# Two attentions over 77 keys: both kinds of scores in one bank per head, on four strips at a time

## The chip, the cores and the metric

The kernel runs on one core of one Trainium2 chip. The metric is the device time of one execution in microseconds; the time shown is the median of three runs.

## The reference, cut to what matters

A decoder of two layers works on x of 8 x 256 tokens x 256 features, with a context of 8 x 77 tokens. Each layer has a self-attention, an attention over the context and a mixture of experts, each followed by a sum and a layer norm. The change touches only the two attentions over the context, which have 16 heads of 16 features. The first (stage L0x) normalises q and k per head and turns q by position:

```python
q = (x @ q_w.T + q_b).reshape(b, s1, H, hd).transpose(0, 2, 1, 3)
kv = (y @ kv_w.T + kv_b).reshape(b, s2, 2, H, hd).transpose(2, 0, 3, 1, 4)
q = _apply_rope(_layernorm(q, qn_w, qn_b)) * scale
k = _layernorm(k, kn_w, kn_b)
attn = softmax(einsum('bhqd,bhkd->bhqk', q, k))          # 256 x 77 a head
o = einsum('bhqk,bhkd->bhqd', attn, v)
return o.reshape(b, s1, c) @ out_w.T + out_b
```

The second (stage L1x) is the same without the norms, the turning and the biases of q, k and v. All is float32.

## The kernel before, in words

One program runs seven stages one after the other; `context_stage` (line 111) builds both L0x and L1x, its kind "rope" or "cross". A stage works through 8 batch entries (blocks, b), each in four steps (st = 0 to 3) of four heads, so n = 4 b + st runs from 0 to 31. The four heads lie on four strips of 32 partitions: `qs` and `keys` have 16 features and a row for the shift in each strip, and a matmul on one strip uses 32 rows of TensorE's array. Every step computes the scores twice.

`scores(n, pair)` (line 527) gives queries on the partitions and keys along the row, for two heads j in the two banks of `psS`, 2 x 77 columns a head; pair 0 and pair 1 use the two halves of the same two banks. When both are there, `row_max(n)` on VectorE (line 829) takes the maximum of each row, with its sign turned, by one reduction for each pair. TensorE transposes these maxima (the item "top"), and `shift(n)` on VectorE (line 842) adds them to the queries, in the row for the shift. `turned_scores(n, half)` (line 548) then computes keys on the partitions and 256 queries along the row, already less the maximum, for two heads in the two banks of `psK`, and `exponential(n, half)` on ScalarE (line 684) takes them to `pT`. `values(n)` (line 559) multiplies by v and `row_sums(n)` (line 571) by ones, both into the bank `psO`, where two steps share a set of 128 output rows. After the second of them `out_norm(o)` on VectorE (line 848) takes the reciprocal of the sums (line 850) and multiplies (line 854). ScalarE and POOL split the result into two parts (`out_high`, `out_low`) for the output projection.

The work that prepares later blocks and closes earlier ones comes in items, each in one of three banks `psF`: transposed x ("xT"), projections ("q", "k", "v", "qT", "kT"), and the output projection ("out", 0 and 1). `slot(n, half)` (line 222) is an order written out by hand: which items stand in the first and the second half of step n. In L1x the second half of each step has the next block's query projection ("qT", line 429), the first half has "xT" at st 0, output projections at st 2 and 3, and in some blocks keys or v at st 1. In L0x the second halves have a query projection (with a bias by line 464), transposes, a v projection in some blocks, and "xT". With the item "top" a few idle matmuls can be issued (`keep_busy`, line 432). In the last blocks most items fall away.

TensorE's order in step n is: turned_scores(n, 0), items of the first slot, values(n - 1), top(n + 1), scores(n + 2, 0), turned_scores(n, 1), row_sums(n - 1), scores(n + 2, 1), items of the second slot. VectorE's is: items of the first slot, shift(n + 1), out_norm(n/2 - 1) if n is even and at least 2, row_max(n + 2), items of the second slot, layer norm. ScalarE's is: exponential(n, 0), items of the first slot, out_high, exponential(n, 1), items of the second slot. All waits are on semaphores counted: `s_max` counts finished row maxima, `p_exp` finished exponentials, `q_shifted` finished shifts.

Of the kernel before, what the change touches and what calls it, by code (L numbers as in the profile page):

```python
# [11 lines left out]
F32 = mybir.dt.float32  # L12
# [8 lines left out]
P = 128  # L21
B = 8
S = 256
# [87 lines left out]
def context_stage(nc, name, kind, consts, x_in, x_out, w):  # L111
# [16 lines left out]
    with ExitStack() as ctx:  # L128
# [59 lines left out]
        psS = ctx.enter_context(nc.psum_tensor(f"{name}_psS", [P, 2, 512], F32))  # L188
        psK = ctx.enter_context(nc.psum_tensor(f"{name}_psK", [P, 2, 512], F32))
# [10 lines left out]
        s_half, s_ready, s_max, q_shifted = sem("s_half"), sem("s_ready"), sem("s_max"), sem("q_shifted")  # L200
# [223 lines left out]
        def _(pe):  # L424
# [102 lines left out]
            def scores(n, pair):  # L527
                b, st = divmod(n, NST)
                if pair == 0:
                    if rope:  # L530
                        for i in range(min(((b + 1) * CTX - 1) // P, CT - 1) + 1):
                            wait_taken(pe, ("kT",), i)
                        wait_taken(pe, ("qT", st // 2), b)
                    else:
                        wait_taken(pe, ("kT", st, b // 4), 0)
                        wait_taken(pe, ("qT", st), b)
                    if n:
                        pe.wait_ge(s_max, n)
                else:
                    pe.wait_ge(s_half, n + 1)  # L540
                for t in range(TT):
                    for j in (2 * pair, 2 * pair + 1):
                        r = slice(32 * j, 32 * j + 32)
                        last = pe.matmul(psS[:, j % 2, (TT * pair + t) * CTX:(TT * pair + t + 1) * CTX],
                                         qs[r, b % 2, st, t * P:(t + 1) * P], keys[r, st, columns(b)], start=True, stop=True)
                last.then_inc(s_half if pair == 0 else s_ready, 1)

            def turned_scores(n, half):
                b, st = divmod(n, NST)
                if half == 0:  # L550
                    pe.wait_ge(q_shifted, n + 1)
                if n or half:
                    pe.wait_ge(p_exp, 2 * n + half)
                for jj in range(2):
                    r = slice(64 * half + 32 * jj, 64 * half + 32 * jj + 32)
                    last = pe.matmul(psK[0:CTX, jj, 0:S], keys[r, st, columns(b)], qs[r, b % 2, st, :], start=True, stop=True)
                last.then_inc(k_ready, 1)

            def values(n):
                b, st = divmod(n, NST)  # L560
                par = st % 2
                pe.wait_ge(p_exp, 2 * n + 2)
                if par == 0 and n >= 2:
                    pe.wait_ge(o_norm, n // 2)
                wait_taken(pe, ("v", b // 2), 0)
                for j in range(4):
                    pe.matmul(psO[32 * j:32 * j + 32, 0:S],
                              vs[0:CTX, b, 4 * (st // 2) + j, 2 * par:2 * par + 2, :].rearrange("p a e -> p (a e)"),
                              pT[0:CTX, n % 2, j, :], start=(par == 0), stop=False)
# [12 lines left out]
            scores(0, 0)  # L582
            scores(0, 1)
            item(("top",), 0)
            scores(1, 0)
            scores(1, 1)
            for n in range(N):
                st = n % NST
                turned_scores(n, 0)
                for what, b in slot(n, 0):  # L590
                    item(what, b)
                if n:
                    values(n - 1)
                if n + 1 < N:
                    item(("top",), n + 1, (1, 0, 2, 0)[st] if rope else (1, 1 if n >= 4 * NST else 0, 0, 0)[st])
                if n + 2 < N:
                    scores(n + 2, 0)
                turned_scores(n, 1)
                if n:
                    row_sums(n - 1)  # L600
                if n + 2 < N:
                    scores(n + 2, 1)
                for what, b in slot(n, 1):
                    item(what, b)
# [6 lines left out]
        def _(act):  # L611
# [72 lines left out]
            def exponential(n, half):  # L684
                act.wait_ge(k_ready, 2 * n + half + 1)
                if half == 0 and n >= 2:
                    act.wait_ge(r_ready, n - 1)
                act.activation(pT[0:CTX, n % 2, 2 * half:2 * half + 2, :], psK[0:CTX, :, 0:S], ACT.Exp).then_inc(p_exp, 1)
# [29 lines left out]
            for n in range(N):  # L718
                st = n % NST
                exponential(n, 0)  # L720
# [5 lines left out]
                exponential(n, 1)  # L726
# [5 lines left out]
        def _(dve):  # L732
# [96 lines left out]
            def row_max(n):  # L829
# [5 lines left out]
                for half in range(2):  # L835
                    last = dve.tensor_reduce(
                        top[:, n % 2, :, 64 * half + HD:64 * half + 64:32].rearrange("p t j -> p j t"),
                        psS[:, :, TT * CTX * half:TT * CTX * (half + 1)].rearrange("p j (t k) -> p j t k", t=TT),
                        AX_X, ALU.max, negate=True)
                last.then_inc(s_max, 1)  # L840
# [2540 lines left out]
```

## Time and profile before

| | us |
|---|---|
| median of 3 runs | 2387.67 |
| lowest, highest | 2387.26, 2424.44 |
| the profiled execution | 2417.0 |
| its span, first to last instruction | 2415.3 |

The profile is that of one execution, on the only core. TensorE's weight loads (PEld) lie beside its matmuls. A float32 matmul stands in the trace as two records, so x8 in a row are four matmuls. PEclk is the share of its full clock that TensorE was granted, 1.00 for 2.4 GHz and 0.50 for 1.2 GHz. An arrow (`<-`) in brackets names what an instruction waited for last.

### The profile page before, as it was taken

To read this page: it belongs to the slowest core of one execution; us is meant where nothing else is said; L and a number is where in the kernel's file an instruction comes from. 1 tells how busy PE (TensorE), PEld (TensorE's weight loads), DVE (VectorE), ACT (ScalarE), POOL (GpSimd) and SP (SyncE) were. 2 spreads that over 40 slices of the span, in tenths; PEclk is the share of its full clock that TensorE was granted. 3 is DMA by queue.
4 is the path that set the end of the run, shared out by engine and by line. 5 is a ranking of instruction groups with operands and counts; after the bars stand their busy time and mean duration, and the time that the engine had idled before them with its cause. 6 is when DMAs were issued, how large, how long until landed. Compare 5 with 4: busy or idle time off the path is not lost. (4 is left out here: it accounts for less than half of the span.)

```text
span 2415.3 us, 39591 instructions
## 1 busy us (share of the span) xinstructions
PE 2064.4 (85%) x15432; PEld 1484.4 (61%) x15432; DVE 1029.0 (43%) x2387; ACT 843.0 (35%) x2148; POOL 650.3 (27%) x607
## 2 busy tenths in 40 slices
PE   5999966998389999389999987995999997899995
PEld 4666755664368888257777765663666665455553
DVE  2556544665323232245555563564356552111112
ACT  3545432342123232335554542432334331122222
POOL 1333334752421321313332331112000000502222
PEclk9999997997589999699999997996799896899998
DMA  1000001000533421600000001002100007412223
GB/s 58 10 10 19 10 14 59 10 23 10 185 93 97 140 80 34 215 1 1 19 10 10 10 10 57 19 19 87 53 14 28 14 28 261 143 36 44 43 42 94
DMA packets 100031, 127.47 MB, mean 53 GB/s; under 512 B 8682, under 2 KB 86970, under 8 KB 99818
## 3 DMA queue, kind: packets, MB, share of 16 engines
q1 hardware_dynamic: 86554, 107.17, 13.5%
q0 software_dynamic: 13296, 17.77, 4.2%
q8 instruction: 128, 2.10, 0.4%
q14 instruction: 53, 0.43, 0.1%
HBM read 87.12 MB, written 39.89 MB: 53 GB/s over the span
## 5 line engine op out<-in xcount | busy, mean ns | idle before, releaser
L2030 POOL TENSOR_TENSOR L1a_probs<-L1a_probs,L1a_rinv 128x1024 f32<-128x1024 f32 x64 | 121.2, 1894 | 286.9 <-DVE L1a_rinv L2360 286.9
L2027 POOL TENSOR_TENSOR L0a_probs<-L0a_probs,L0a_rinv 128x256 f32<-128x256 f32 (+1 forms) x128 | 103.1, 826 | 219.7 <-DVE L0a_rinv L2360 219.7
L2351 DVE CUSTOM_DVE_ANT_0 L1a_sbias<-L1a_psS,L1a_bias 128x256 f32<-128x256 f32 x256 | 93.2, 421 | 124.0 <-PE L1a_psS L2164 124.0
L2279 ACT ACTIVATE L1a_probs<-L1a_sbias,L1a_nmx 128x256 f32<-128x256 f32 x256 | 126.5, 497 | 40.0 <-DVE L1a_nmx L2351 40.0
L3229 DVE TENSOR_TENSOR moe_h<-moe_h,moe_psU 128x512 f32<-128x512 f32 x55 | 37.8, 688 | 226.4 <-PE moe_psU L3048 200.7
L2784 DVE TENSOR_TENSOR ec_hT<-ec_sg,ec_psU 128x512 f32<-128x512 f32 x64 | 44.0, 688 | 194.3 <-ACT ec_sg L2714 194.3
L2999 POOL DMA_INDIRECT moe_sums<-moe_y,moe_xg x39 | 60.8, 1559 | 234.8 <-DVE moe_y L3241 231.9
L2655 PE MATMUL ec_psA<-ec_wd,ec_hT 128*128 128x256 f32 x512 | 112.6, 381 | 5.2 <-DVE ec_hT L2784 5.2
L2279 ACT ACTIVATE L0a_probs<-L0a_psS,L0a_nmx 128x128 f32<-128x128 f32 (+1 forms) x256 | 104.0, 422 | 36.7 <-DVE L0a_nmx L2342 36.7
L2590 POOL DMA_INDIRECT ec_sums<-ec_yk,ec_token_at x32 | 50.4, 1574 | 228.6 <-ACT ec_yk L2722 223.8
L3070 PE MATMUL moe_psY<-moe_wts,moe_hT 128*128 (+1 forms) x440 | 106.0, 384 | 6.1 <-issue 5.3
L3070 PEld LDWEIGHTS moe_psY<-moe_wts,moe_hT 128*128 128x128 f32 x440 | 84.4, 193 | 41.3 <-issue 32.4
L2655 PEld LDWEIGHTS ec_psA<-ec_wd,ec_hT 128*128 128x128 f32 x512 | 96.6, 190 | 20.1 <-DVE ec_hT L2784 7.3
L1564 ACT ACTIVATE L1s_pT<-L1s_psK 128x1024 f32<-128x1024 f32 x64 | 65.6, 1024 | 106.2 <-PE L1s_psK L1428 106.2
L2643 PE MATMUL ec_psG<-ec_xs,ec_wt 128*128 128x512 f32 x384 | 100.4, 397 | 2.1 <-issue 2.1
L3129 ACT ACTIVATE moe_hT<-moe_psH 128x512 f32<-128x512 f32 x55 | 32.8, 597 | 191.0 <-PE moe_psH L3062 171.4
L2643 PE MATMUL ec_psU<-ec_xs,ec_wt 128*128 128x512 f32 x384 | 98.8, 393 | 0.0
L2342 DVE TENSOR_REDUCE L0a_nmx<-L0a_psS 128x2 f32<-128x256 f32 (+1 forms) x128 | 65.3, 552 | 72.4 <-PE L0a_psS L2161 72.4
L1724 DVE TENSOR_REDUCE L1s_top<-L1s_psS 128x8 f32<-128x2048 f32 x32 | 73.2, 2288 | 32.2 <-PE L1s_psS L1414 32.2
L2367 DVE COPY L1a_pT<-L1a_psT 128x1024 f32<-128x1024 f32 x64 | 78.2, 1222 | 19.9 <-PE L1a_psT L2179 19.9
L2714 ACT ACTIVATE ec_sg<-ec_psG 128x512 f32<-128x512 f32 x64 | 38.3, 598 | 137.4 <-PE ec_psU L2643 133.2
L2051 PE MATMUL L1a_psF<-L1a_xT,L1a_wq 128*128 128x256 f32 x384 | 64.8, 306 | 23.4 <-DVE L1a_xT L2377 17.7
(485 smaller groups left out, 4776.9 us busy)
## 6 DMA issues: line engine op xcount, KB each, us to landing
ec_wg<-in_L_ffn_w_gate SPq DMA_DIRECT2D x8, 1024.0 KB
ec_wu<-in_L_ffn_w_up SPq DMA_DIRECT2D x8, 1024.0 KB
ec_wd<-in_L_ffn_w_down SPq DMA_DIRECT2D x8, 1024.0 KB, 5.6
moe_rows<-blank SPq DMA_DIRECT2D x1, 5070.0 KB, 20.9
moe_xg<-moe_rows SPq DMA_DIRECT2D x39, 130.0 KB, 2.1
moe_wts<-in_L_ffn_e_gate SPq DMA_DIRECT2D x8, 512.0 KB
moe_wts<-in_L_ffn_e_up SPq DMA_DIRECT2D x8, 512.0 KB
moe_wts<-in_L_ffn_e_down SPq DMA_DIRECT2D x8, 512.0 KB
```

Of the source, the lines that this page charges most:

```text
L1564: act.activation(pT[0:KP, n % 2, 2 * half:2 * half + 2, :], psK[0:KP, :, 0:KT * S], ACT.Exp).then_inc(p_exp, 1)
L1724: last = dve.tensor_reduce(top[:, n % 2, :, HD::32].rearrange("p t j -> p j t"), psS[:].rearrange("p j (t k) -> p j t k", t=TT), AX_X, ALU ...
L2027: last = pool.tensor_tensor(v, v, bcast(rinv[:, r, :, t], 2, KEYS[t]), ALU.mult)
L2030: last = pool.tensor_tensor(v, v, bcast(rinv[:, r, :, :].rearrange("p h t -> p (h t)"), 2, S), ALU.mult)
L2051: last = pe.matmul(out, l(a), r(c), start=(start and j + k == 0), stop=(stop and 3 * j + k == n - 1))
L2279: ins = act.activation(probs[:, r, j, at:at + KEYS[t]], src[:, at:at + KEYS[t]], ACT.Exp, bias=nmx[:, r, j, t:t + 1], scale=1.0 if latent ...
L2342: last = dve.tensor_reduce(nmx[:, r, :, t], psS[:, slot:slot + 2, P * t:P * t + KEYS[t]], AX_X, ALU.max, negate=True)
L2351: last = dve.tensor_tensor_reduce(out=sbias[:, g % 2, j, t * S:(t + 1) * S], in0=psS[:, slot + j, t * S:(t + 1) * S], in1=bias[:, 2 * (g % ...
L2367: dve.tensor_copy(pT[:, g % 2, :, :].rearrange("p j (k r c) -> p r (j k) c", r=2, c=64), psT[:, :, 0:PW].rearrange("p r (n c) -> p r n c", ...
L2643: last = pe.matmul(ps[:, i % 2, :], wt[:, a, j, c, i * P:(i + 1) * P], xs[:, b, c, :], start=(n == 0), stop=(n == len(products) - 1))
L2655: last = pe.matmul(psA[:, half, s % 2 * D:(s % 2 + 1) * D], hT[:, i, s * P:(s + 1) * P], wd[:, e % 2, i, :], start=(i == 0), stop=(i == IC ...
L3070: last = pe.matmul(psY[:, 0:D], hT[:, g % 2, f, :], weights(e, 2)[:, f * D:(f + 1) * D], start=(f == 0), stop=(f == FC - 1))
```

## The change

Both stages get the same edit. One tile `psX` of four banks, one for each head j of a step, takes the place of `psS` and `psK`. The left part of a bank (154 columns) holds the scores, columns 256 to 511 the turned scores. Scores, turned scores, the exponential and the row maxima of a step are no longer split into pairs: the loops over j run over all four strips, and ScalarE and VectorE have one instruction each. Since both kinds share banks, `scores(n)` also waits for the exponential of n - 2 (`p_exp` at n - 1) and `turned_scores(n)` also waits for the row maxima of n + 1 (`s_max` at n + 2). TensorE's order becomes: turned_scores(n), values(n - 1), items of the first slot, top(n + 1), scores(n + 2), row_sums(n - 1), items of the second slot. The order on VectorE is unchanged.

```diff
--- before.py
+++ after.py
@@ -185,8 +185,7 @@
             wqk = sb("wqk", [P, 2, KD, 2, NST, 4, 32], F32R)
             row16 = sb("row16", [P, 1])
 
-        psS = ctx.enter_context(nc.psum_tensor(f"{name}_psS", [P, 2, 512], F32))
-        psK = ctx.enter_context(nc.psum_tensor(f"{name}_psK", [P, 2, 512], F32))
+        psX = ctx.enter_context(nc.psum_tensor(f"{name}_psX", [P, 4, 512], F32))
         psO = ctx.enter_context(nc.psum_tensor(f"{name}_psO", [P, 512], F32))
         psF = ctx.enter_context(nc.psum_tensor(f"{name}_psF", [P, NF, 512], F32))
 
@@ -197,7 +196,7 @@
         x_in_sem = [sem(f"x_in{n}") for n in range(RX)]
         item_ready, item_high = sem("item_ready"), sem("item_high")
         item_taken = [sem(f"item_taken{n}") for n in range(NF)]
-        s_half, s_ready, s_max, q_shifted = sem("s_half"), sem("s_ready"), sem("s_max"), sem("q_shifted")
+        s_ready, s_max, q_shifted = sem("s_ready"), sem("s_max"), sem("q_shifted")
         k_ready, p_exp = sem("k_ready"), sem("p_exp")
         r_ready, r_inverse, o_norm, o_high, o_low = sem("r_ready"), sem("r_inverse"), sem("o_norm"), sem("o_high"), sem("o_low")
         ln_step, rs_asked, rs_done = sem("ln_step"), sem("rs_asked"), sem("rs_done")
@@ -524,42 +523,42 @@
                                               for c in range(KD)])
                 last.then_inc(item_ready, 1)
 
-            def scores(n, pair):
+            def scores(n):
                 b, st = divmod(n, NST)
-                if pair == 0:
-                    if rope:
-                        for i in range(min(((b + 1) * CTX - 1) // P, CT - 1) + 1):
-                            wait_taken(pe, ("kT",), i)
-                        wait_taken(pe, ("qT", st // 2), b)
-                    else:
-                        wait_taken(pe, ("kT", st, b // 4), 0)
-                        wait_taken(pe, ("qT", st), b)
-                    if n:
-                        pe.wait_ge(s_max, n)
+                if rope:
+                    for i in range(min(((b + 1) * CTX - 1) // P, CT - 1) + 1):
+                        wait_taken(pe, ("kT",), i)
+                    wait_taken(pe, ("qT", st // 2), b)
                 else:
-                    pe.wait_ge(s_half, n + 1)
+                    wait_taken(pe, ("kT", st, b // 4), 0)
+                    wait_taken(pe, ("qT", st), b)
+                if n:
+                    pe.wait_ge(s_max, n)
+                if n >= 2:
+                    pe.wait_ge(p_exp, n - 1)
                 for t in range(TT):
-                    for j in (2 * pair, 2 * pair + 1):
+                    for j in range(4):
                         r = slice(32 * j, 32 * j + 32)
-                        last = pe.matmul(psS[:, j % 2, (TT * pair + t) * CTX:(TT * pair + t + 1) * CTX],
+                        last = pe.matmul(psX[:, j, t * CTX:(t + 1) * CTX],
                                          qs[r, b % 2, st, t * P:(t + 1) * P], keys[r, st, columns(b)], start=True, stop=True)
-                last.then_inc(s_half if pair == 0 else s_ready, 1)
-
-            def turned_scores(n, half):
+                last.then_inc(s_ready, 1)
+
+            def turned_scores(n):
                 b, st = divmod(n, NST)
-                if half == 0:
-                    pe.wait_ge(q_shifted, n + 1)
-                if n or half:
-                    pe.wait_ge(p_exp, 2 * n + half)
-                for jj in range(2):
-                    r = slice(64 * half + 32 * jj, 64 * half + 32 * jj + 32)
-                    last = pe.matmul(psK[0:CTX, jj, 0:S], keys[r, st, columns(b)], qs[r, b % 2, st, :], start=True, stop=True)
+                pe.wait_ge(q_shifted, n + 1)
+                if n:
+                    pe.wait_ge(p_exp, n)
+                if n + 1 < N:
+                    pe.wait_ge(s_max, n + 2)
+                for j in range(4):
+                    r = slice(32 * j, 32 * j + 32)
+                    last = pe.matmul(psX[0:CTX, j, S:2 * S], keys[r, st, columns(b)], qs[r, b % 2, st, :], start=True, stop=True)
                 last.then_inc(k_ready, 1)
 
             def values(n):
                 b, st = divmod(n, NST)
                 par = st % 2
-                pe.wait_ge(p_exp, 2 * n + 2)
+                pe.wait_ge(p_exp, n + 1)
                 if par == 0 and n >= 2:
                     pe.wait_ge(o_norm, n // 2)
                 wait_taken(pe, ("v", b // 2), 0)
@@ -579,27 +578,22 @@
 
             for what, b in FRONT:
                 item(what, b, 14 if rope and (what, b) == (("qT", 0), 0) else 0)
-            scores(0, 0)
-            scores(0, 1)
+            scores(0)
             item(("top",), 0)
-            scores(1, 0)
-            scores(1, 1)
+            scores(1)
             for n in range(N):
                 st = n % NST
-                turned_scores(n, 0)
+                turned_scores(n)
+                if n:
+                    values(n - 1)
                 for what, b in slot(n, 0):
                     item(what, b)
-                if n:
-                    values(n - 1)
                 if n + 1 < N:
                     item(("top",), n + 1, (1, 0, 2, 0)[st] if rope else (1, 1 if n >= 4 * NST else 0, 0, 0)[st])
                 if n + 2 < N:
-                    scores(n + 2, 0)
-                turned_scores(n, 1)
+                    scores(n + 2)
                 if n:
                     row_sums(n - 1)
-                if n + 2 < N:
-                    scores(n + 2, 1)
                 for what, b in slot(n, 1):
                     item(what, b)
             values(N - 1)
@@ -681,11 +675,11 @@
                 act.wait_ge(o_in, 32)
                 act.activation(wo[:, 0, :, :], raw_o[:], ACT.Copy).then_inc(w_high, 1)
 
-            def exponential(n, half):
-                act.wait_ge(k_ready, 2 * n + half + 1)
-                if half == 0 and n >= 2:
+            def exponential(n):
+                act.wait_ge(k_ready, n + 1)
+                if n >= 2:
                     act.wait_ge(r_ready, n - 1)
-                act.activation(pT[0:CTX, n % 2, 2 * half:2 * half + 2, :], psK[0:CTX, :, 0:S], ACT.Exp).then_inc(p_exp, 1)
+                act.activation(pT[0:CTX, n % 2, :, :], psX[0:CTX, :, S:2 * S], ACT.Exp).then_inc(p_exp, 1)
 
             def out_high(o):
                 act.wait_ge(o_norm, o + 1)
@@ -717,13 +711,12 @@
                         high_o()
             for n in range(N):
                 st = n % NST
-                exponential(n, 0)
+                exponential(n)
                 for what, at in slot(n, 0):
                     if what[0] != "out":
                         take(what, at)
                 if st % 2 == 1 and n >= 3:
                     out_high(n // 2 - 1)
-                exponential(n, 1)
                 for what, at in slot(n, 1):
                     take(what, at)
             out_high(N // 2 - 1)
@@ -832,12 +825,9 @@
                     dve.wait_ge(item_ready, ready(("top",), n - 2))
                 if n == 0:
                     dve.wait_ge(zeroed, 3)
-                for half in range(2):
-                    last = dve.tensor_reduce(
-                        top[:, n % 2, :, 64 * half + HD:64 * half + 64:32].rearrange("p t j -> p j t"),
-                        psS[:, :, TT * CTX * half:TT * CTX * (half + 1)].rearrange("p j (t k) -> p j t k", t=TT),
-                        AX_X, ALU.max, negate=True)
-                last.then_inc(s_max, 1)
+                dve.tensor_reduce(top[:, n % 2, :, HD::32].rearrange("p t j -> p j t"),
+                                  psX[:, :, 0:TT * CTX].rearrange("p j (t k) -> p j t k", t=TT),
+                                  AX_X, ALU.max, negate=True).then_inc(s_max, 1)
 
             def shift(n):
                 b, st = divmod(n, NST)
```

## Rows read from the trace of the kernel before

**Rows 1.** Part 1 of the page: busy time of each engine, share, instructions.
```profile
PE 2064.4 (85%) x15432; PEld 1484.4 (61%) x15432; DVE 1029.0 (43%) x2387; ACT 843.0 (35%) x2148; POOL 650.3 (27%) x607
```

**Rows 2.** Stretches of L0x and L1x: us, busy per engine, PEclk, DMA share, GB/s.
```profile
480.00:500.00 20.00, 20.00 (x203) 13.23 (x196) 13.75 (x29) 8.89 (x19) 12.88 (x13) 1.00 0.09 27
1558.00:1641.00 83.00, 82.41 (x860) 53.23 (x858) 48.95 (x103) 32.71 (x64) 13.65 (x16) 1.00 0.07 21
```

**Rows 3.** Timeline of one step of L1x: start us, us, engine, line, operation.
```profile
1567.18 0.34 PE L544 MATMUL L1x_psS<-L1x_keys,L1x_qs 32*128 32x77 f32 x2
...
1567.80 0.64 PE L576 MATMUL L1x_psO<-L1x_pT,L1x_ones 77*32 77x256 f32 x8
...
1568.37 0.67 PE L544 MATMUL L1x_psS<-L1x_keys,L1x_qs 32*128 32x77 f32 x8
1568.50 1.76 DVE L850 RECIPROCAL L1x_rinv<-L1x_psO 128x256 f32<-128x256 f32 x1 [0.79 <-PE L1x_psO L576]
...
1568.97 0.97 PE L429 MATMUL L1x_psF<-L1x_xT,L1x_wqk 128*128 128x256 f32 x6
...
1569.87 0.66 PE L556 MATMUL L1x_psK<-L1x_qs,L1x_keys 32*77 32x256 f32 x4
...
1570.46 0.97 PE L429 MATMUL L1x_psF<-L1x_wo,L1x_oT 128*128 128x256 f32 x6
1570.58 0.59 ACT L688 ACTIVATE L1x_pT<-L1x_psK 77x512 f32<-77x512 f32 x1
1570.64 0.86 DVE L836 TENSOR_REDUCE L1x_top<-L1x_psS 128x4 f32<-128x308 f32 x2
...
1571.36 0.64 PE L567 MATMUL L1x_psO<-L1x_pT,L1x_vs 77*32 77x256 f32 x8
...
1571.93 0.44 PE L518 MATMUL L1x_psF<-ident,L1x_top 128*128 128x128 f32 x2
...
1572.30 0.34 PE L544 MATMUL L1x_psS<-L1x_keys,L1x_qs 32*128 32x77 f32 x2
```

**Rows 4.** Groups by line and shape, 1490 to 1644 us: busy us, mean ns, idle before.
```profile
L688 ACT ACTIVATE L1x_pT<-L1x_psK 77x512 f32<-77x512 f32 x59 | 35.0, 594 | 49.4 <-PE L1x_psK L556 46.0
...
L836 DVE TENSOR_REDUCE L1x_top<-L1x_psS 128x4 f32<-128x308 f32 x60 | 25.8, 473 | 22.3 <-PE L1x_psS L544 22.3
```

**Rows 5.** Part 5 of the page: two rows of the stage L1s, wider tiles.
```profile
L1564 ACT ACTIVATE L1s_pT<-L1s_psK 128x1024 f32<-128x1024 f32 x64 | 65.6, 1024 | 106.2 <-PE L1s_psK L1428 106.2
...
L1724 DVE TENSOR_REDUCE L1s_top<-L1s_psS 128x8 f32<-128x2048 f32 x32 | 73.2, 2288 | 32.2 <-PE L1s_psS L1414 32.2
```

**Rows 6.** Timeline of a step of L0x, around its query projection.
```profile
492.34 0.70 PE L464 MATMUL L0x_psF<-L0x_rows,ident 128*128 128x256 f32 x2
...
493.68 0.66 PE L556 MATMUL L0x_psK<-L0x_qs,L0x_keys 32*77 32x256 f32 x4
```

**Rows 7.** Timeline of the last block of L1x, where values wait.
```profile
1641.27 1.76 DVE L850 RECIPROCAL L1x_rinv<-L1x_psO 128x256 f32<-128x256 f32 x1 [0.79 <-PE L1x_psO L576]
...
1643.59 0.64 PE L567 MATMUL L1x_psO<-L1x_pT,L1x_vs 77*32 77x256 f32 x8 [1.47 <-ACT L1x_pT L688]
```

**Rows 8.** Stretches of L1x and L1s, columns as in rows 2.
```profile
1641.00:1644.40 3.40, 1.93 (x25) 0.98 (x22) 3.10 (x5) 1.33 (x3) 0.58 (x2) 1.00 0.00 0
1644.40:1660.00 15.60, 15.60 (x98) 7.72 (x101) 6.73 (x15) 3.38 (x6) 1.77 (x3) 0.50 0.05 18
1804.80:1808.20 3.40, 3.40 (x26) 2.15 (x24) 0.69 (x1) 0.00 (x0) 0.00 (x0) 0.50 0.00 0
1808.20:1815.00 6.80, 6.80 (x69) 4.65 (x66) 4.07 (x4) 2.04 (x3) 0.00 (x0) 1.00 0.02 4
```

**Rows 9.** Timeline of TensorE at the end of L1x.
```profile
1654.06 1.14 PE L556 MATMUL L1x_psK<-L1x_qs,L1x_keys 32*77 32x256 f32 x4
...
1655.13 1.65 PE L429 MATMUL L1x_psF<-L1x_wo,L1x_oT 128*128 128x256 f32 x6
...
1656.71 0.66 PE L567 MATMUL L1x_psO<-L1x_pT,L1x_vs 77*32 77x256 f32 x4
```

## The prediction, made before the changed kernel was run

> **What bounds the kernel now.** The page of the profile comes first: TensorE is busy 2064 us of the span of 2415.3 us, twice as long as any other engine [rows 1]. A share over the whole span says little about one stage, so the stretches come next. The change touches two stages of seven, the attentions over the 77 context keys, L0x (about 411 to 600 us) and L1x (about 1489 to 1660 us). In a stretch of 20 us of L0x and one of 83 us of L1x TensorE is busy all but 0.6 us, VectorE 59 to 69% and ScalarE 39 to 44% of the time, and the granted clock is 1.00, the 2.4 GHz level [rows 2]. The timeline of one step shows what that means. Each row there is a group of matmuls, and the distance from one start to the next is what a group costs TensorE: scores of the first pair of heads with turned scores of the second pair (started together) 0.62 us (1567.18 to 1567.80), row sums 0.57, scores of the second pair 0.60, the next block's query projection 0.90, turned scores of the first pair 0.59, output projection 0.90, values 0.57, transpose of the maxima 0.37, together 5.12 us, and the next step begins at 1572.30 with no wait between any two [rows 3]. So TensorE's stream of groups sets the time of a step, and the waits fit beneath it. They fit narrowly. In every second step VectorE takes the reciprocal at 1568.50 and then the product, and only 2.14 us later the maxima, which end at 1571.50. The first group that needs them is the transpose, at 1571.93: 0.43 us to spare [rows 3].
>
> **The change part by part, on TensorE.** Turned scores: two groups of two strips become one of four. Four strips side by side are already in the trace: the mixed group of 0.62 us holds scores on strips 0 and 1 and turned scores on strips 2 and 3, each strip with a bank of its own, and costs hardly more than either half alone (0.60, 0.59) [rows 3]. I take 0.60 for four turned strips and 0.62 for four strips of scores. If nothing ran together beyond two strips it would be 1.18 and 1.20. Before, a step had 0.62 + 0.60 + 0.59 = 1.81 us of these; after, 1.22. That saves 0.59 us a step, 38 us over 64 steps, for as long as TensorE's stream is the bound.
>
> The page "TensorE: Matmul & The Clock Gate" of the Trainium skill, section "Measured speedup vs the span model", gives 3.07 times and not 4 times for four row tiles. By it a four-strip group would cost 1.3 times a lone strip, which would add about 0.35 us to a step, 23 us in all. The mixed group here does not show this loss, so the sum leaves it out.
>
> **On ScalarE and VectorE.** Two exponentials of 512 columns at 594 ns become one of 1024 [rows 4]; another stage has a row of 1024 columns at 1024 ns [rows 5]. I take 1.02 us (bounds 0.59 and 1.19). Two maxima of 308 columns at 473 ns become one of 616. Between the rows of 308 and 2048 columns (2288 ns) the slope is 1.04 ns a column, so 0.79 us (bounds 0.47 and 0.95) [rows 4, 5]. ScalarE has slack, so its gain is worth nothing by itself.
>
> **The waits, which are the costly part.** Before, the maxima read one pair of banks and the exponentials another. Now every bank has scores on the left and turned scores on the right, so TensorE may write neither while VectorE or ScalarE reads the other. The two added waits: scores(n+2) wait for exponential n, and turned scores(n+1) wait for the maxima of n+2. Behind each stands all of TensorE's queue, values, projections and transposes, and behind these the shift on VectorE and the exponential on ScalarE.
>
> First wait, from the start of the turned group to the start of scores. TensorE has 0.60 + 0.57 values + 0.90 projection + 0.37 transpose = 2.44 us to issue. The exponential starts 0.71 us after its group (1569.87 to 1570.58), takes 1.02 and releases TensorE about 0.12 later (the distance between a group's issue and its reader, 0.71 less 0.59): 1.85 us [rows 3, 5]. It is hidden. In a step with no item in the first slot TensorE has only 1.54 us, and some 0.3 us show.
>
> Second wait, from the start of scores to the next turned group. TensorE has 0.62 + 0.57 row sums + 0.90 projection = 2.09 us. In odd steps the maxima end at 0.62 + 0.12 + 0.79, plus 0.12: 1.65 us, hidden. In even steps the reciprocal stands ahead of the maxima in VectorE's order and waits for the row sums, which now follow the scores of all four strips. The way is 0.62 scores, 0.70 until the reciprocal starts (1567.80 to 1568.50), 2.14 until the maxima start, 0.79 for them, 0.12 to release: 4.37 us against 2.09. TensorE stands still for 2.28 us. Before, turned scores, output projection and values, 2.06 us, lay ahead of the first group that needed the maxima; the change puts them behind it.
>
> Two steps then take 2.44 + 4.37 + 2.44 + 2.09 = 11.34 us against 10.24: 1.10 us more. A reciprocal waits in 15 pairs of a stage (one each for n = 2, 4 to 30): 16 us for L1x. Steps without an output item are shorter in both kernels and change this by tenths; I keep 15. In L0x the query group after the scores takes 1.34 us (492.34 to 493.68) [rows 6], so that the stall is 1.84 us, and in the other even step the slot is empty in most blocks (stall 4.37 less 1.19, 3.2 us) or holds a value projection that covers nearly all of it. I take 2.0 us on average, less 2 x 0.59: 0.8 us a pair, 12 us. At full clock the change costs 27 us.
>
> **The clock.** The trace of before has such stalls where the last blocks have no items left. The reciprocal starts at 1641.27, and values wait until 1643.59, of which 1.47 us are idle beyond the end of the earlier matmuls [rows 7]. The stretch from 1641.0 to 1644.4 still has the clock at 1.00 with TensorE busy 1.93 of 3.40 us; the following 15.6 us have it at 0.50, the 1.2 GHz level [rows 8]. At that level a turned group costs 1.07 us (1654.06 to 1655.13) and an output projection 1.58 (to 1656.71) against 0.59 and 0.90 [rows 3, 9], a factor of 1.78. In another stage a low stretch lasts only 3.4 us and the clock is back [rows 8]. So the low stretch lies between 3.4 and 15.6 us, and I take 6, nearer to the row where work is again dense. The two steps at the low level: 2.44 and 2.09 times 1.78 are 4.34 and 3.72; the even way is (0.62 + 0.57) x 1.78 + 0.14 + 2.14 + 0.79 + 0.12 = 5.31; together 17.7 us instead of 11.34. Time at the low level thus loses 36%. If three stalls of four lower the clock: 30 x 0.75 x 6 x 0.36 = 49 us. The ends are nothing, and all pairs low, 30 x (17.7 - 10.24) = 224 us.
>
> **The sum.** 27 + 49 = 76 us. The profiled execution took 2417 us around its span of 2415.3 (profiled 1.2% above the median of the runs), so it would become 2493; against the median of 2387.67, 2464 us. No DMA, no weight load outside the groups and nothing on the POOL queue is added; the groups that are moved within a step keep their dependencies, apart from the waits above.
>
> **The rivals.**
> Clock holds: the stalls come, but TensorE's groups on either side are dense enough. For it: 0.8 to 3.2 us is no long pause, and the stretches of L0x and L1x hold 1.00 [rows 2]. Against it: a shorter stall than mine stands ahead of the fall in the trace [rows 7, 8]. It costs 27 us: 2415.
> Low clock nearly everywhere: the next stall comes some 11 us after the last, so the clock may not come back, as it did not for 15.6 us [rows 8]. With seven tenths of the time low a pair takes about 15.2 us: 30 x 5.0 = 150 us, 2538; all low, 2612.
> Not slower: VectorE's reciprocal is less in the way than I reckon, and the saving of TensorE comes through. The place is the second wait in even steps, and it decides at a stall of 2 x 0.59 = 1.18 us; below that the change gains, up to 38 us without any stall: 2350, and 2370 with half of it. For it, TensorE's stream is the bound today; against it, the spare today is 0.43 us and the cover that goes is 2.06.
> Strips don't run by fours: 0.6 us more in each of the two groups, on the way of both waits. Besides the stalls that is up to 77 us: 2540. The mixed group speaks against it.
>
> **How the numbers follow.** Forecast 0.60, clock holds 0.22, low nearly everywhere 0.08, not slower 0.06, strips 0.04. 2% of the median, 48 us, is about what a measurement of this kernel can tell from no change. The forecast's own spread (low stretches of 4 to 10 us) is 2436 to 2500, so a part of it, 0.03, stays within 2%. Faster by over 2%: 0.02; within 2%: 0.22 + 0.04 + 0.03, 0.29; slower: 0.69. The range reaches down to the case of the clock that holds, 2408, and up to the low clock most of the time, 2535.
>
> **What would show it.** Right: turned scores on four strips at about 0.60 us a group; one exponential at about 1.02 us and one row of maxima at 0.79; in even steps an idle of about 2.3 us ahead of the turned scores, put down to the maxima; granted clock of 0.5 in stretches of L0x and L1x, which grow from 189 us (L0x) and 171 us (L1x) by about 38 us each. Wrong: both stages shorter than before, TensorE's groups still without a gap, or four-strip groups above 1 us at the full clock.

## The result, and the profile after

The changed kernel takes 2476.51 us (median of 4 runs, 2474.71 to 2479.52) against 2391.96 us for the kernel before (4 runs): a ratio of 1.036, 95% interval 1.033 to 1.038, so 3.6% slower. The forecast was 2464 us, 3.2% over the median then known.

Part 1 of the page of the changed kernel answers to [rows 1]. TensorE has the same 15432 instructions, VectorE and ScalarE have 64 fewer each:

```profile
PE 2077.3 (84%) x15432; PEld 1485.9 (60%) x15432; DVE 1021.3 (41%) x2323; ACT 832.1 (34%) x2084; POOL 650.1 (26%) x607
```

The windows view, cut from the first exponential of a stage to the last, says where the time went. First the kernel before (columns as in [rows 2]: length, busy time of TensorE, weight loads, VectorE, ScalarE, POOL, then the granted clock):

```profile
412.10:598.20 186.10, 178.59 (x1682) 113.48 (x1685) 110.94 (x226) 68.48 (x138) 95.12 (x89) 0.90 0.05 14
1490.60:1658.90 168.30, 165.72 (x1650) 105.45 (x1654) 94.37 (x191) 64.22 (x123) 24.28 (x29) 0.95 0.05 16
```

and the changed kernel:

```profile
411.10:619.70 208.60, 175.50 (x1660) 109.67 (x1660) 103.28 (x187) 62.65 (x106) 94.01 (x87) 0.82 0.04 13
1511.90:1735.80 223.90, 192.57 (x1628) 118.32 (x1628) 86.90 (x152) 57.88 (x90) 23.01 (x27) 0.69 0.04 12
```

L0x has grown by 22.5 us and L1x by 55.6, together 78.1. The mean granted clock has fallen from 0.90 to 0.82 and from 0.95 to 0.69. Since the clock has only two levels, its distance from 1.00, doubled, is the share of the stage at 1.2 GHz: 37 and 17 us before, 75 and 139 us after, 160 us more in all. All other stages together took 17 us less in this execution than in the profiled one of before (2417.0 us, 25 above its median); their code is the same in both kernels.

Length less busy time is TensorE's idle time: 10.1 us in both stages together before, 64.4 after.

The timeline of TensorE in L0x shows the groups at the full clock. Four turned strips take 0.60 us (495.93 to 496.53), the scores of four strips 0.62 (497.94 to 498.56), and then comes the wait, 2.21 us, put down to the maxima on line 828:

```profile
495.93 0.67 PE L555 MATMUL L0x_psX<-L0x_qs,L0x_keys 32*77 32x256 f32 x8
496.53 0.64 PE L566 MATMUL L0x_psO<-L0x_pT,L0x_vs 77*32 77x256 f32 x8
...
497.94 0.68 PE L542 MATMUL L0x_psX<-L0x_keys,L0x_qs 32*128 32x77 f32 x16
498.56 0.64 PE L575 MATMUL L0x_psO<-L0x_pT,L0x_ones 77*32 77x256 f32 x8
...
502.74 0.67 PE L555 MATMUL L0x_psX<-L0x_qs,L0x_keys 32*77 32x256 f32 x8 [2.21 <-DVE L0x_top L828]
```

The even step of L1x answers to [rows 3]. The row sums start at 1570.62, the reciprocal 0.70 us later, the maxima 2.13 us after it, and TensorE starts 0.15 us after their end:

```profile
1569.79 0.89 PE L542 MATMUL L1x_psX<-L1x_keys,L1x_qs 32*128 32x77 f32 x16
...
1570.62 0.64 PE L575 MATMUL L1x_psO<-L1x_pT,L1x_ones 77*32 77x256 f32 x8
...
1571.32 1.76 DVE L840 RECIPROCAL L1x_rinv<-L1x_psO 128x256 f32<-128x256 f32 x1 [1.00 <-PE L1x_psO L575]
...
1573.45 0.79 DVE L828 TENSOR_REDUCE L1x_top<-L1x_psX 128x8 f32<-128x616 f32 x1
...
1574.39 1.15 PE L555 MATMUL L1x_psX<-L1x_qs,L1x_keys 32*77 32x256 f32 x8 [2.24 <-DVE L1x_top L828]
```

The groups by line and shape in L1x answer to [rows 4]. One exponential of 1024 columns takes 1.02 us, one row of maxima over 616 columns 0.80:

```profile
L682 ACT ACTIVATE L1x_pT<-L1x_psX 77x1024 f32<-77x1024 f32 x32 | 32.6, 1020 | 59.6 <-PE L1x_psX L555 59.6
...
L828 DVE TENSOR_REDUCE L1x_top<-L1x_psX 128x8 f32<-128x616 f32 x31 | 24.7, 797 | 8.7 <-PE L1x_psX L542 8.7
```

The waits of TensorE there (total us, times, longest) have one row that matters, 15 waits and 31.9 us; in L0x it is 17 waits and 31.3 us:

```profile
PE L1x_psX L555 <- DVE L1x_top L828: 31.9, 15, 3.1
```

The windows around the wait of the timeline above: TensorE is busy in 1.96 of 3.40 us, at the full clock (0.99), and the 30.8 us that follow are at 0.50. The clock had come back only at 1570.2, after a low stretch that ended with 3.40 us of unbroken work.

```profile
1566.80:1570.20 3.40, 3.40 (x24) 2.12 (x20) 0.95 (x2) 1.41 (x2) 0.08 (x1) 0.50 0.00 0
1570.20:1573.60 3.40, 1.96 (x30) 1.26 (x26) 2.37 (x4) 0.47 (x1) 0.00 (x0) 0.99 0.00 0
1573.60:1604.40 30.80, 28.45 (x194) 17.11 (x195) 9.90 (x20) 7.33 (x11) 3.39 (x4) 0.50 0.06 18
```

### The profile page after: what moved, and what is told of

Read it like the earlier page. It is cut to its first block and busy times, and to the rows that moved or that the text cites. A ratio compares the mean times of both kernels' runs of the same rounds, so it can differ in the third digit from the quotient of the medians.

```text
span 2476.0 us, 39509 instructions
## 1 busy us (share of the span) xinstructions
PE 2077.3 (84%) x15432; PEld 1485.9 (60%) x15432; DVE 1021.3 (41%) x2323; ACT 832.1 (34%) x2084; POOL 650.1 (26%) x607
## 5 line engine op out<-in xcount | busy, mean ns | idle before, releaser
L1554 ACT ACTIVATE L1s_pT<-L1s_psK 128x1024 f32<-128x1024 f32 x64 | 65.5, 1024 | 102.8 <-PE L1s_psK L1418 102.8
L2633 PEld LDWEIGHTS ec_psG<-ec_xs,ec_wt 128*128 128x128 f32 x384 | 72.8, 190 | 17.5 <-issue 2.4
```

Of the source, the lines that this page charges most:

```text
L1554: act.activation(pT[0:KP, n % 2, 2 * half:2 * half + 2, :], psK[0:KP, :, 0:KT * S], ACT.Exp).then_inc(p_exp, 1)
L2633: last = pe.matmul(ps[:, i % 2, :], wt[:, a, j, c, i * P:(i + 1) * P], xs[:, b, c, :], start=(n == 0), stop=(n == len(products) - 1))
```

## The experiments

The ratio compares each run with the kernel before on the same chip. The runs come from several chips: the median of the kernel before was 2392.0 us beside the changed kernel, 2394.8 beside e1 to e4, 2395.2 beside e5 to e8 and 2400.1 beside e9 and e10, so differences in us between these sets of runs are good to some 8 us. The stage lengths, from first to last exponential, and the clocks are those of the one profiled execution.

| run | median us | ratio to before | L0x, L1x us | mean clock in L0x, L1x |
|---|---|---|---|---|
| changed kernel | 2476.5 | 1.036 (1.033 to 1.038) | 208.6, 223.9 | 0.82, 0.69 |
| e1, the stall filled | 2400.3 | 1.002 (0.999 to 1.004) | 182.6, 169.5 | 0.97, 1.00 |
| e2, maxima first | 2385.0 | 0.996 (0.994 to 0.999) | 180.2, 161.6 | 0.90, 0.93 |
| e3, before, maxima first | 2463.4 | 1.031 (1.025 to 1.037) | 206.3, 218.7 | 0.83, 0.73 |
| e4, copy for reciprocal | 2373.5 | 0.993 (0.989 to 0.996) | 175.2, 154.7 | 0.90, 0.97 |
| e5, sums before scores | 2448.3 | 1.021 (1.017 to 1.026) | 195.8, 207.3 | 0.87, 0.72 |
| e6, e2 and values moved | 2333.4 | 0.974 (0.971 to 0.978) | 152.1, 138.5 | 0.97, 0.99 |
| e7, e6 with split reads | 2334.5 | 0.974 (0.971 to 0.977) | 153.9, 140.4 | 0.96, 0.99 |
| e8, e6 with busy ends | 2334.5 | 0.977 (0.973 to 0.980) | 157.7, 140.0 | 0.98, 0.99 |
| e9, before with both moves | 2377.9 | 0.988 (0.981 to 0.996) | 178.4, 158.8 | 0.90, 0.95 |
| e10, e6 with scores by pairs | 2323.9 | 0.966 (0.959 to 0.973) | 152.3, 138.1 | 0.97, 1.00 |

**e1: wait or clock?** The changed kernel, with idle matmuls where TensorE waits:

```diff
+            def fill(n):
+                b, st = divmod(n - 1, NST)
+                if not slot(n - 1, 1):
+                    many = 6
+                else:
+                    many = (4 if not rope else 3 if st == 0 else 0)
...
+                keep_busy(bank(*nxt), many)
             for n in range(N):
+                if n >= 3 and n % 2 == 1:
+                    fill(n)
                 turned_scores(n)
```

> The changed kernel with idle matmuls in the place where TensorE waits for the row maxima: 4 ahead of the turned scores of each odd step in L1x, 3 or none in L0x, 6 where the slot before is empty. Theory (about a third of the loss is the wait, the rest the lower clock that the wait brings on): the wait stays but TensorE is not idle, the granted clock is 1.00 over nearly all of both stages, and the time falls to before + 27 us, 2419 (2405 to 2435). Rival (the lower clock costs little, because VectorE's chain sets the pace anyway; the whole loss is waiting): 2465 to 2480 as the changed kernel, whatever the clock does.

The windows of both stages, and the wait that is left in L1x:

```profile
409.90:592.50 182.60, 169.99 (x1762) 111.17 (x1762) 102.51 (x187) 62.67 (x106) 94.03 (x87) 0.97 0.05 14
1483.60:1653.10 169.50, 160.72 (x1744) 105.79 (x1744) 85.96 (x152) 57.90 (x91) 23.09 (x27) 1.00 0.05 15
```

```profile
PE L1x_psX L571 <- DVE L1x_top L846: 8.5, 16, 1.0
```

L1x is at 1.00 from end to end, and of the 84.5 us over the kernel before 5.5 are left (2400.3 against 2394.8 on the same chip), though every even step is still as long as VectorE makes it: the idle matmuls compute nothing, they only run in the pause. Against the changed kernel both stages are 80.4 us shorter with 203 us less at the low level (214 against 11), 0.40 us for each. The rival, that the clock matters little, is out. The time lies 19 us below the estimate and below its range. Two things account for it. e1 has 43 us less at the low level than the kernel before (11 against 54), which is an estimated 17 us at 0.40 each. And the cost at the full clock was put too high: from the second block of L1x to the eighth, where both kernels run at 1.00, six blocks take 137.9 us in e1 (first shift at 1499.47, then 1637.37) and 128.1 in the kernel before (1507.26, 1635.36). That is 0.82 us for each pair of steps, where 1.10 had been forecast.

**e2: the order on VectorE.**

```diff
+                if n + 2 < N:
+                    row_max(n + 2)
                 if st % 2 == 0 and n >= 2:
                     out_norm(n // 2 - 1)
-                if n + 2 < N:
-                    row_max(n + 2)
```

> The changed kernel with two lines of VectorE's order exchanged: row_max(n + 2) ahead of out_norm(n/2 - 1). Theory (the reciprocal ahead of the maxima is the whole stall): the second wait takes 0.62 + 0.12 + 0.79 + 0.12 = 1.65 us in every step and is hidden under 2.09, the clock stays at 1.00, TensorE's saving of 0.59 us a step comes through: 2388 - 38 = 2350 us (2340 to 2368), faster than both. Rival (one set of banks for both kinds of scores is too tight in any order): stalls of over 0.5 us a step stay, 2420 or more.

Some 92 us faster than the changed kernel by one exchange, so the place of the stall is shown: the reciprocal ahead of the maxima. But it is 35 us above the expectation and outside its range. The timeline of L1x has the reason:

```profile
1549.98 0.67 PE L555 MATMUL L1x_psX<-L1x_qs,L1x_keys 32*77 32x256 f32 x8
...
1551.40 0.42 DVE L844 TENSOR_TENSOR L1x_oN<-L1x_psO,L1x_rinv 128x256 f32<-128x256 f32 x1
...
1551.93 0.64 PE L566 MATMUL L1x_psO<-L1x_pT,L1x_vs 77*32 77x256 f32 x8 [1.28 <-ACT L1x_pT L682]
```

The wait has moved to the values of every second step. They write the bank that VectorE's product reads, and the product now comes after the maxima. I had checked the maxima against their reader and not the product against its own. The profile names the exponential as the releaser, but that had ended at 1547.24: values also wait for the product's semaphore, and the product ended at 1551.82. L1x has 14 such pauses, 15.8 us in all.

**e3: the same exchange in the kernel before**, where scores and turned scores have banks of their own.

> The kernel before with the same exchange on VectorE. It is the control for e2. Theory: TensorE's groups follow one another without a gap there, so only the waits of the last blocks (1.9 us each) and the stretches of low clock behind them go: 2372 to 2388. Rival (the order on VectorE alone is what gains in e2, and the four strips bring nothing): as e2, near 2350.

Both expectations failed: the kernel before becomes 3.1% slower. The pause of e2 appears, here 1.65 us ahead of values (1608.69). VectorE cannot start the maxima before the scores of the second pair are there (1605.49) and does the reciprocal only behind them, so the product ends at 1608.59:

```profile
1606.39 1.75 DVE L850 RECIPROCAL L1x_rinv<-L1x_psO 128x256 f32<-128x256 f32 x1
...
1608.17 0.42 DVE L854 TENSOR_TENSOR L1x_oN<-L1x_psO,L1x_rinv 128x256 f32<-128x256 f32 x1
...
1608.69 0.92 PE L567 MATMUL L1x_psO<-L1x_pT,L1x_vs 77*32 77x256 f32 x8 [1.65 <-ACT L1x_pT L688]
```

```profile
412.20:618.50 206.30, 191.08 (x1682) 120.61 (x1686) 110.20 (x226) 68.55 (x139) 95.18 (x89) 0.83 0.04 13
1503.80:1722.50 218.70, 207.02 (x1650) 129.20 (x1654) 93.19 (x191) 64.70 (x123) 24.01 (x29) 0.73 0.04 12
```

From these windows the low level holds for 70 us of L0x and 118 of L1x, 134 us more than before, and both stages together are 70.6 us longer. At 0.40 us each, 54 of them are the clock's; TensorE's idle time has grown by 17 (from 10.1 to 26.9), which is the rest. So the kernel before shows the same thing without four strips and without banks shared by both kinds of scores: a few pauses in TensorE's stream cost far more than their length. L1x has nine, 11.6 us in all. After the five of 0.59 to 0.75 us the clock stayed at 1.00; each of the three of 1.64 or 1.65 us stands at the start of a low stretch.

**e4: a shorter way through VectorE.**

```diff
-                dve.reciprocal(rinv[:, o % 2, :], psO[:, S:2 * S]).then_inc(r_inverse, 1)
+                dve.tensor_copy(rinv[:, o % 2, :], psO[:, S:2 * S]).then_inc(r_inverse, 1)
```

> The changed kernel with a copy in place of the reciprocal (it leaves out the division, so the sums are not inverted); 0.42 us instead of 1.76. Theory (the stall is as long as the way through VectorE, and a shorter one spares the clock): the stall ahead of the turned scores in even steps falls from 2.25 to 0.9 us, below the 1.18 at which the change breaks even, few falls of the clock, 2380 to 2400. Rival (any pause in TensorE's stream at these places lowers the clock): stretches at 0.50 stay nearly as many, 2430 or more.

This kernel leaves out the division. At 2373.5 us it is a little faster than the expected range.

```profile
PE L1x_psX L555 <- DVE L1x_top L828: 14.6, 15, 1.8
```

```profile
1475.40:1630.10 154.70, 139.93 (x1632) 87.77 (x1635) 67.53 (x153) 57.96 (x91) 23.11 (x27) 0.97 0.05 17
```

The same 15 waits, 14.6 us instead of 31.9, and L1x has one low stretch at its end. The length of the stall is VectorE's way, and in L1x pauses of about 1.0 us did not bring the low level. L0x stays at 0.90, as before the change, with 13 such waits of 15.1 us in all.

**e5: the row sums ahead of the scores on TensorE.**

```diff
-                if n + 2 < N:
-                    scores(n + 2)
                 if n:
                     row_sums(n - 1)
+                if n + 2 < N:
+                    scores(n + 2)
```

> The changed kernel with the row sums issued ahead of the scores instead of behind them. The reciprocal then starts 0.62 us earlier against the scores, so the wait ahead of the turned scores in even steps should be 1.65 us instead of 2.25. Theory (loss = full-clock part + 0.38 us for each us at the low clock): some 15 us from the shorter wait and some of the low clock gone, 2420 to 2455. Rival (the order on TensorE does not matter because the maxima wait for something else): 2470 to 2480, and the same wait.

```profile
PE L1x_psX L555 <- DVE L1x_top L828: 22.3, 15, 2.1
```

```profile
1500.10:1707.40 207.30, 184.16 (x1628) 112.54 (x1628) 86.75 (x152) 57.99 (x90) 23.04 (x27) 0.72 0.04 13
```

The 15 waits have shrunk from 31.9 to 22.3 us, 0.64 us each, where 0.60 had been reckoned. The clock in L1x stays at 0.72, so most of its part of the loss is still there, and the time is in the upper half of the expected range. With e4 and e1 this gives a scale for the 15 or 16 pauses of L1x by their mean length: 1.0 us, clock 0.97; 1.5 us, 0.72; 2.1 us, 0.69; 2.1 us filled down to 0.5, 1.00. It holds for this order only: e3 comes to 0.73 with nine pauses of 11.6 us in all.

**e6: both moves.** e2, and values behind the scores, so that the product on VectorE has time:

```diff
                 turned_scores(n)
-                if n:
-                    values(n - 1)
...
                     scores(n + 2)
                 if n:
+                    values(n - 1)
                     row_sums(n - 1)
```

> e2 and, on TensorE, values(n - 1) moved from ahead of the first slot to behind scores(n + 2). In e2 the wait had only moved: values of every second step waited 1.28 us for the product of VectorE. Here the product has 1.9 us of projection and transpose and 0.6 of scores more to be ready. Theory: no wait over 0.3 us is left in the inner blocks, a block of L1x takes 20.6 - 4 x 0.58 = 18.3 us at the full clock, both stages together 25 us shorter than in e2: ratio to before 0.980 to 0.988 (2347 to 2366). Rival (the first wait now shows, since only 1.87 us cover its 1.85, and TensorE's pauses return there): 2375 to 2390 as e2.

2.6% faster than before, 5.9% faster than the changed kernel (0.974 against 1.036), and a little more than expected: the ratio lies below 0.980 to 0.988, and both stages are 51 us shorter than in e2, not 25. Eight rows of L1x, one step from scores to scores, and the windows of both stages:

```profile
1500.21 0.68 PE L542 MATMUL L1x_psX<-L1x_keys,L1x_qs 32*128 32x77 f32 x16
...
1500.82 0.64 PE L566 MATMUL L1x_psO<-L1x_pT,L1x_vs 77*32 77x256 f32 x8
...
1501.28 0.61 PE L575 MATMUL L1x_psO<-L1x_pT,L1x_ones 77*32 77x256 f32 x8
...
1501.82 0.97 PE L428 MATMUL L1x_psF<-L1x_xT,L1x_wqk 128*128 128x256 f32 x6
...
1502.72 0.67 PE L555 MATMUL L1x_psX<-L1x_qs,L1x_keys 32*77 32x256 f32 x8
...
1503.33 0.97 PE L428 MATMUL L1x_psF<-L1x_wo,L1x_oT 128*128 128x256 f32 x6
...
1504.13 0.38 PE L517 MATMUL L1x_psF<-ident,L1x_top 128*128 128x128 f32 x2
...
1504.63 0.68 PE L542 MATMUL L1x_psX<-L1x_keys,L1x_qs 32*128 32x77 f32 x16
```

```profile
414.80:566.90 152.10, 143.45 (x1661) 97.37 (x1662) 102.69 (x187) 61.76 (x106) 94.19 (x87) 0.97 0.06 17
1452.90:1591.40 138.50, 133.26 (x1629) 90.22 (x1629) 85.39 (x152) 57.14 (x90) 23.05 (x27) 0.99 0.06 19
```

The step takes 4.42 us (1500.21 to 1504.63) against 5.12 in [rows 3], and no group waits. The saving is 0.70 us, where 0.59 had been reckoned. The groups of scores give the 0.59. The rest comes from values that stand directly ahead of the row sums: 0.46 and 0.54 us instead of 0.57 and 0.57. The output projection (0.80 instead of 0.90) and the transpose (0.50 instead of 0.37) nearly cancel. Of the rival's wait little shows: scores wait six times for the exponential in L1x, 3.3 us in all.

**e7: one instruction or two.** e6 with exponential and maxima cut in two again, on the same four banks.

> e6 with exponential and maxima in two instructions each again, on the same four banks, so that only this part of the change is undone. Theory: the exponential takes 0.17 us more and its cover is used up, so 0.1 to 0.2 us a step show, 5 to 12 us over e6. Rival (VectorE and ScalarE have slack, one or two instructions are the same): within 3 us of e6.

1.1 us apart with overlapping intervals: the rival held. The wait of the theory is there, but small: in L1x scores wait 18 times for the exponential, 5.5 us in all, against 6 times and 3.3 us in e6, and both stages together are 3.6 us longer. In e6's order, "one instruction per step" for these reads is worth nothing that the time of the kernel can show.

**e8: idle matmuls where a slot is empty** (e6 with two ahead of the turned scores wherever the slot before is empty).

> e6 with 2 idle matmuls ahead of the turned scores wherever the second slot before is empty (some steps of L0x, the last block of both). Theory: the low stretches in the last blocks and in the last blocks of L0x go, about 15 us of low clock at 0.38 each less 1 us for the matmuls: 3 to 8 us below e6. Rival (the ends are paced by the chain through VectorE and ScalarE, which the clock does not touch, and the idle matmuls only delay): equal to or 2 to 6 us above e6.

No gain, 1.1 us apart again, as the rival said. L0x is even 5.6 us longer in the profiled execution: TensorE is busy there for 150.6 us instead of 143.5, while its waits are no longer than in e6. So the idle matmuls themselves make the difference; their price had been put at 1 us. The clock had little to give back: 0.98 against 0.97 in L0x, 0.99 in L1x in both.

**e9: the moves alone**, in the kernel before: maxima ahead of the reciprocal, values behind turned scores of the second pair and ahead of the row sums.

> The kernel before (two sets of banks, pairs of strips) with both moves of e6: maxima ahead of the reciprocal, values behind the first scores. Theory (the stream of TensorE is the bound there, so an order without waits gains only the low stretches of the last blocks): the inner blocks of L1x stay at 20.6 to 22 us, whole time 2370 to 2392. Rival (the order alone makes the gain of e6, four strips bring little): 2345 or less, blocks near 18 us.

```profile
1483.80:1642.60 158.80, 156.67 (x1642) 108.06 (x1645) 90.25 (x188) 63.43 (x124) 23.70 (x28) 0.95 0.05 16
```

The gain is 1.2% (0.4 to 1.9). In the trace the fifth block of L1x, from its first shift to that of the next block, takes 19.4 us; it had been expected to stay at 20.6, as in the kernel before, and is 17.7 in e6. All three ran at the full clock there. So of 2.9 us a block 1.2 come from the order and 1.7 from the change itself. Four strips in one group should give 4 x 0.59 = 2.4; some 0.7 of it goes again ahead of the scores, which start 0.48 us behind the start of the transpose in e6 and 0.31 in e9 (medians over L1x).

**e10: the loop over the strips.** e6 with the scores issued by pairs of strips.

```diff
-                for t in range(TT):
-                    for j in range(4):
+                for pair in range(2):
+                    for t in range(TT):
+                        for j in (2 * pair, 2 * pair + 1):
```

> e6 with the loops of the scores by pairs of strips again, all else kept, so that only two strips run beside each other. Theory (four strips side by side are the gain): the group of scores takes 1.1 to 1.2 us instead of 0.62, 0.5 to 0.6 us a step more, 30 to 37 us over 64 steps: 2360 to 2372. Rival (TensorE overlaps the second pair with the first through its queue anyway): the group stays below 0.8 us, 2333 to 2345.

```profile
1503.68 0.70 PE L543 MATMUL L1x_psX<-L1x_keys,L1x_qs 32*128 32x77 f32 x16
...
1504.31 0.64 PE L567 MATMUL L1x_psO<-L1x_pT,L1x_vs 77*32 77x256 f32 x8
```

The group takes 0.63 us (1503.68 to 1504.31) against 0.61: the rival held, and the time lies below even its range (2323.9 against 2333 to 2345), on another chip than e6; both stages together are as long as in e6 (290.4 against 290.6). Two pairs one behind the other would be 1.2 us by the price of one pair (0.60), so the second pair runs beside the first whatever the order in the loop. In the kernel before, other groups stood between the pairs.

## Why the prediction was right

**The bound and the saving.** TensorE's stream was the bound, and four-strip groups take 0.60 and 0.62 us, as the step "turned scores" took them from the mixed group. The page "TensorE: Matmul & The Clock Gate" of the Trainium skill, section "Measured speedup vs the span model", gives 3.07 times and not 4 for four row tiles. From two strips (0.59 and 0.60 us) to four (0.60 and 0.62) nothing of such a loss shows here; against a lone strip it can't be compared, since none runs alone in these stages.

**The first wait** was hidden, as said: 0.3 us in all of L1x. **The second wait** has the place, the releaser and the size of the forecast: 2.24 us in the step shown, against 2.28. The exponential (1.02) and the maxima (0.80 against 0.79) fit as well. Over both stages the stalls were put at 15 x 2.28 + 15 x 2.0 = 64 us, and they measure 63.2 (31.9 and 31.3). That this wait is caused by the reciprocal ahead of the maxima is shown by e2, e4 and e5, from three sides.

**The clock.** The forecast was 49 us, as 30 stalls, three of four with a fall, 6 us at the low level each (135 us of it), and 36% lost of that time. Measured: 160 us more at the low level, 0.40 us lost for each, 64 us. Both factors were somewhat too small. The low stretches are fewer and longer than forecast: in the granted clock of the trace both stages have 21 of them, of about 10 us on average, against 6 in the kernel before; the forecast had 22.5 new ones of 6 us. That number and length missed in opposite ways is luck. e1 shows that it is the clock and not the wait that carries the most.

**The full-clock part** was put at 27 us. (Its parts, 16 and 12, make 28.) What the stages lost beyond the 64 us is 78.1 - 64 = 14 us. The idle time says nearly the same without the clock: 54.3 us more of it, less the 38 saved, is 16. The forecast was too high here because it set 64 us of stalls against nothing, where the kernel before had 10.1 us of idle time already, and because a pair of steps costs 0.82 us more in L1x and not 1.10 (e1). So the sum of 76 (against 84.5 by the medians) holds two errors of opposite sign, and it came as near as it did by luck; the ratio of the terms was not 1 to 2 but 1 to 4 or 5. The lower end of the spread does not follow from its terms either: low stretches of 4 us give 27 + 32, so 2447, not 2436. L0x and L1x were given like shares; L1x has 71% of the loss, with 139 us at the low level against 75.

**What was not seen.** That the exchange on VectorE would only move the wait to values (e2), and that it would harm the kernel before (e3): in both the reader of the maxima was followed and the reader of the product was not.

## What to carry to other kernels

Where an engine's stream is the bound and looks full, list for each group the time at which its input is there: the slack (here 0.43 us) says more than the busy share, and a change that lets two readers share a bank moves waits ahead of groups that used to cover them. When two results come out of one engine, place each by its own first reader, both of them. And a pause in TensorE's stream has a second price by its clock, which here was several times the first, in the changed kernel (64 us against 14) as in the kernel before with one exchange (e3, 54 against 17).

## What the runs showed of the hardware that was not expected

The low level can outlast the pause ahead of it by far. In the changed kernel the clock stayed at 0.50 for 30.8 us, but there a second pause, of 1.56 us, falls into the stretch after 15.9 us of unbroken work. The clearest case is in e3, behind the pause of 1.65 us at 1608.69: TensorE works without a gap and the clock is still low for 40 us. What ends such a stretch was not tried, and stays open.

```profile
1605.30:1608.70 3.40, 1.75 (x17) 1.13 (x14) 3.06 (x5) 1.14 (x3) 0.00 (x0) 1.00 0.00 0
1609.80:1650.20 40.40, 40.40 (x238) 25.28 (x240) 12.85 (x27) 8.62 (x17) 3.44 (x5) 0.50 0.07 20
```

What a group costs TensorE depends on its neighbours. Values and row sums (77 rows, 32 columns, four column strips) take 0.45 to 0.46 and 0.54 to 0.55 us side by side (medians of some 30 steps in each of e6, e7 and e10), 0.57 each when groups of other shapes stand between them. The output projection takes 0.80 to 0.82 us ahead of the transpose, which has its shape (128*128), and 0.90 ahead of values. That the same shape is the cause is likely but was not tested by itself. Values and row sums give 0.14 us a step, 0.56 of the 1.2 us a block that the order alone gained in e9.

Strips run beside each other although they are issued pair after pair (e10): 0.63 us against 0.61 for 16 matmul records, and 0.60 for the 8 of one pair alone.
